# A graph-network kernel whose gathers signal VectorE: each group's five VectorE operations begin on that signal, in another order, and the sums are copied with a lag of one group

## What is computed

```
h = maximum(layernorm(x), 0)
eq = h @ Wq + bq
ek = h @ Wk + bk
e = edge_attr @ We + be
m = relu(eq[dst] + ek[src] + e)
ft = segment_sum(m, dst, num_segments=6250)
out = x + ft @ Wr + br
```

## Time and profile before

| what | value |
|---|---|
| median of 3 runs | 1306.76 us (1306.44 to 1307.97) |
| profiled execution, first to last instruction | 1303.3 us |
| edge phase in it, first gather to last | 118.4 to 1230.8 us |
| busy in the whole span | PE 1153.0, DVE 964.9, ACT 841.4, POOL 948.3 us |
| DMA | 303.48 MB, mean 233 GB/s |

### The profile page before, as it was taken

How to read it: one execution, slowest core, us unless ns; L and a number is a source line. 1 busy time by engine, 2 the same in 40 slices (tenths; PEclk the granted TensorE clock), 3 DMA queues, 4 the chain that set the end, 5 groups by cost and what they waited for, 6 DMA issues and landing times.

```text
span 1303.3 us, 33240 instructions
## 1 busy us (share of the span) xinstructions
PE 1153.0 (88%) x8632; PEld 1056.0 (81%) x8632; DVE 964.9 (74%) x1324; ACT 841.4 (65%) x1463; POOL 948.3 (73%) x946
## 2 busy tenths in 40 slices
PE   2997899999999999999989898999999989999776
PEld 2776888888888888888888888888888888888766
DVE  6885777777777777777777777777777777777688
ACT  2775676666666666666666666666666666666533
POOL 4545777777777777777777777777777777777644
PEclk9998999999999999999999999999999999999989
DMA  8887877777777777777777777777777777777564
GB/s 263 287 285 245 248 230 233 230 233 230 235 234 244 228 235 231 235 233 233 237 233 235 233 232 232 232 232 231 230 235 234 242 224 240 230 233 232 191 188 149
DMA packets 164469, 303.48 MB, mean 233 GB/s; under 512 B 29204, under 2 KB 110740, under 8 KB 164452
## 3 DMA queue, kind: packets, MB, share of 16 engines
q1 hardware_dynamic: 124516, 194.18, 45.7%
q0 software_dynamic: 39936, 109.11, 28.8%
HBM read 275.69 MB, written 27.48 MB: 233 GB/s over the span
## 4 chain that ended last, share of the span: by engine, by line
POOL 53%; issue 32%; PE 8%; DVE 3%; DMA 2%; POOLq 1%; ACT 1%; DVEq 0%; SPq 0%; ACTq 0%
POOL k_rows L492 53%; PE p_sum L926 4%; PE p_edge L926 3%; DVE hT_lo L888 1%; DMA ft<-in_x 1%; PE p_turn L935 1%; POOLq L499 0%; POOLq L237 0%; DMA pre<-in_dst_groups 0%; DMA range_table<-top_g 0%; DVE k_rows L900 0%; DMA rel_row<-rel_table 0%; DMA k_rows<-k_table,idx 0%; DVE k_rows L715 0%; POOLq L490 0%
## 5 line engine op out<-in xcount | busy, mean ns | idle before, releaser
L492 POOL DMA_INDIRECT k_rows<-k_table,idx x832 | 859.1, 1033 | 256.1 <-issue 255.5
L926 PE MATMUL p_edge<-we_hi,edge_hi 128*128 128x256 f32 x1664 | 487.5, 293 | 27.0 <-issue 17.9
L835 DVE TENSOR_TENSOR pre<-p_edge,k_rows 128x1024 f32<-128x1024 f32 x208 | 254.6, 1224 | 300.9 <-issue 155.4
L926 PE MATMUL p_edge<-we_lo,edge_hi 128*128 128x256 f32 x1664 | 466.4, 280 | 0.0
L926 PE MATMUL p_edge<-we_hi,edge_lo 128*128 128x256 f32 x1664 | 466.0, 280 | 0.0
L612 ACT ACTIVATE m_hi<-pre 128x1024 fp32r<-128x1024 f32 x208 | 221.0, 1062 | 352.0 <-DVE pre L835 351.8
L926 PEld LDWEIGHTS p_edge<-we_hi,edge_hi 128*128 128x128 f32 x1664 | 315.3, 189 | 61.2 <-issue 57.4
L926 PEld LDWEIGHTS p_edge<-we_lo,edge_hi 128*128 128x128 f32 x1664 | 316.1, 190 | 0.0
L926 PEld LDWEIGHTS p_edge<-we_hi,edge_lo 128*128 128x128 f32 x1664 | 314.1, 189 | 0.0
L843 DVE SCALAR_TENSOR_TENSOR m_lo<-pre,m_hi 128x1024 fp32r<-128x1024 f32 x208 | 254.3, 1223 | 1.7 <-ACT m_hi L612 1.7
L816 DVE TENSOR_TENSOR edge_lo<-edge,edge_hi 128x1024 fp32r<-128x1024 f32 x208 | 252.7, 1215 | 0.9 <-ACT edge_hi L591 0.9
(11 more groups left out here) (81 smaller groups left out, 961.1 us busy)
## 6 DMA issues: line engine op xcount, KB each, us to landing
edge<-in_edges SPq DMA_DIRECT2D x208, 512.0 KB
rel_row<-rel_table SPq DMA_DIRECT2D x208, 96.0 KB
q_win<-q_table SPq DMA_DIRECT2D x416, 48.0 KB
q_table<-m_hi SPq DMA_DIRECT2D x52, 256.0 KB, 2.5
k_rows<-k_table,idx POOLq DMA_INDIRECT x832
ft<-in_x SPq DMA_DIRECT2D x4, 1664.0 KB, 11.8
k_table<-k_rows SPq DMA_DIRECT2D x52, 128.0 KB, 3.0
out_rows<-k_rows SPq DMA_DIRECT2D x13, 512.0 KB, 3.2
```

The costliest lines, as they stand in the source:

```text
L492: nc.gpsimd.indirect_dma_start(out=k_rows[:, slot, j, :], out_offset=None, in_=k_table, in_offset=bass.IndirectOffsetOnAxis(ap=idx[:, slot ...
L835: nc.vector.tensor_tensor(pre[:, slot % 2, :], p_edge[:, slot % 2, :], k_rows[:, slot].rearrange("p t d -> p (t d)"), ALU.add).then_inc(s_ ...
L926: ins = nc.tensor.matmul(target, a(h), b[:, h, :], start=(h == 0 and n == 0), stop=(stop and h == HALVES - 1 and n == 2))
```

## The change

```diff
+LEAD = 2
+        s_wrote = sem("gather_descriptors_written")
...
                     nc.gpsimd.indirect_dma_start(
                         out=k_rows[:, slot, j, :], out_offset=None, in_=k_table,
                         in_offset=bass.IndirectOffsetOnAxis(ap=idx[:, slot, j:j + 1], axis=0),
+                        engine_sem=s_wrote,
                     ).then_inc(s_rows[slot], 16)
...
                     message_high(it, u)
                     if not (last and u + 2 >= UNROLL):
                         make_pick(it, u + 2)
-                    if not (first and u < 2):
-                        take_sum(it, u - 2)
+                    if not (first and u < 1):
+                        take_sum(it, u - 1)
...
             steps(bodies - 1, last=True)
-            take_sum(bodies - 1, UNROLL - 2)
             take_sum(bodies - 1, UNROLL - 1)
...
-            def add_rows(it, u):
+            def add_rows(it, u, last=False):
                 body, slot, n, _, _ = visit(it, u)
 
+                if not (last and u + LEAD >= UNROLL + 1):
+                    dve.wait_ge(s_wrote, TILES * (n + LEAD))
                 after(dve, s_prod, n)
                 dve.wait_ge(s_rows[slot], 16 * TILES * (body + 1))
                 after(dve, s_mlo, n - 2)
...
             def steps(it, first=False, last=False):
                 for u in range(UNROLL):
-                    add_rows(it, u)
+                    add_rows(it, u, last)
+                    make_send(it, u)
+                    if not (first and u < 3):
+                        add_sum(it, u - 3)
                     if not (last and u + 2 >= UNROLL):
                         edge_low(it, u + 2)
-                    make_send(it, u)
                     message_low(it, u)
-                    if not (first and u < 3):
-                        add_sum(it, u - 3)
```

## The result

The changed kernel takes 1419.4 us (median of 4 runs, 1418.28 to 1419.53), the kernel before beside it 1306.6 us (median of 4, 1306.1 to 1307.97). The ratio is 1.0862, interval 1.0846 to 1.0878: 8.6% slower. The forecast of 1275 us and its range up to 1310 were wrong. The rival "the signal is too early", priced at 1424 us, is what happened.

What follows compares the result with a forecast made beforehand. POOL's 832 back-to-back gathers were taken as the bound, 5.35 us per group. A mean period of 5.19 us saved 33 us, 2 us came back: 1306.8 - 31 = 1275 us, range 1260 to 1310.

Steps and rivals of the forecast that it cites:

- the signal is too early: Rival on the new wait: p under 0.055 us lets `m_lo` hold up third gathers; 115 us more, 1424 us; chance 0.19.
- What s is: Step estimating when `pre` starts after the awaited gather: 0.17 us, giving a period of 5.05 us, bounds 5.03 to 5.21.
- p: Time from a gather's profiled end until POOL counts it as finished; taken as 0.14 us, possible from 0 to 0.305.
- s: Start of `pre` on DVE, counted from the end of the fourth gather whose signal it awaits; taken as 0.17 us.
- steps 1 to 3: Edge-loop steps where the wait stands on `pre` itself; predicted period 5.05 us each.
- The contention: DVE operation with two SBUF inputs running 0.05 us into a gather delays its end to 0.83 us after that operation; 66 us overall.
- No contention to be won: Rival from the skill's inference: DVE's order would not matter to gathers, time about 1308 us; chance 0.02.
- The seam: Point between `edge_lo` and `m_lo` where the third gather comes in; needs s over 0.085 us.
- The period: Time per group of four gathers: the larger of 5.03 us and s + 4.88 us.
- step 0: Edge-loop step with its wait three instructions ahead of `pre` and late `edge_lo`, 0.27 us each; predicted 5.59 us.
- the rest: Side effects: ACT's copy lag costs nothing, PE stays 0.14 us short of bounding, 2 us added once at the end.
- the late rival: Rival on the new wait: p of 0.22 to 0.305 us uses up the gain, 1293 to 1309 us; chance 0.18.

Runs made afterwards that it cites:

- wait-last kernel: Changed kernel, new wait behind `pre`'s others, one instruction after it in steps 1 to 3: full 1254.9 us; light (16 of 24 edge-product matmuls left out) 1255.1 us.
- light counting: Kernel before without 16 of its 24 edge-product matmuls, gathers counted in `s_wrote` and nobody waiting: 1314.0 us, ratio 1.0053 to the full kernel before.

## Why the prediction was wrong

**The step that failed is "What s is".** It took p = 0.14 us between a gather's profiled end and the signal, and so s = 0.17. In the changed kernel `pre` starts 0.033 us (0.032 to 0.034 in steps 1 to 3) after the gather's end. The way to DVE alone, 0.03 us by the earlier trace rows for an ordinary POOL operation, accounts for all of that, and less than 0.01 us is left for p. The row I went by has POOL's sequencer at its next instruction 0.14 us after a gather's end; the signal reaches DVE 0.1 us before that, so the row bears on something else. Rows 6 spoke for the early signal with the very number, and got 0.19.

Everything that hangs on s was right, once s is put in:

- **The contention** (a look soon after the start, an end 0.83 us after the DVE operation's). Gathers of 1.965, 1.65, 1.10, 1.00 and 1.13 us in four kernels end where it says. Only the look at 0.05 us is too strict for an operation that does not follow another with two SBUF inputs: the second gather of the changed kernel has `edge_lo` begin 0.04 us after its start (707.82 against 707.78) and stays at 0.95 us. The Trainium skill, "SBUF — State Buffer", section "Who interferes with whom", infers that `tensor_tensor` does not hold up descriptor writing. The traces do not agree for these gathers: with `edge_lo`, a `tensor_tensor`, running at its start the gather takes 1.65 in place of 0.95 us. "No contention to be won" fell with it.
- **The seam**, s over 0.085. s = 0.033 loses it and s = 0.145 keeps it. No kernel had an s between the two, but the 0.05 us on which the threshold rests is borne out by the other seams above.
- **The period** s + 4.88: 5.12 measured for s = 0.245, and for step 0 of the wait-last kernel 0.033 + 0.27 + 4.88 = 5.18 against 5.206. For the lost seam 6.05 was priced, 6.043 measured; step 0 5.46, measured 5.480.
- **`edge_lo` after `pre`**: 1.58 and in step 0 1.85; measured 1.571 and 1.858. The three instructions ahead of `pre` in step 0: 0.27; measured 0.312 - 0.033 = 0.28.
- **The sum of the rival**: 208 x 5.90 = 1227 us of edge phase, measured 1225.0.

Of "the rest": counting is free, shown by light counting. That PE is not the bound at 5.03 us is shown by the two wait-last kernels, light and full, with the same time, though PE leads the chain of the full one. The 2 us at the end did not come: from the last gather's end to the last instruction it takes 72.6 us after and 72.5 before. `pre` of the last group is 0.7 us later, not 2: it starts 3.5 us after the last gather's end, and before it started 2.8 after it, where the prediction had about 2. Behind it, the shorter lag leaves three `ft` after the last `m_lo` in place of four, which the prediction did not count. The lag of ACT's copy was not tried alone; nor was the new order alone on a chip where POOL bounds.

The weighing of the late rival was wrong as well: 0.18 for p of 0.22 to 0.305 rested on "the 0.30 us gap must hold something". Whatever it holds, the signal does not wait for it.

## What to carry to other kernels

A wait that lines one engine up with another fixes a phase between them, and a fixed phase repeats its luck in every round: the old order lost 0.32 us per group to the contention, the new one 1.01 us in three groups of four. When a result turns on a few hundredths of a microsecond, price both sides of the edge, take the signal's delay from the nearest completion of the same engine and not from what its sequencer does next, and put in a cheap instruction to move the phase before giving the idea up. That a change is slower may mean that it stands 0.1 us from its best place.

## What the runs showed of the hardware

- The completion of a gather reaches a waiting DVE operation 0.033 us after its profiled end, while the next gather starts 0.305 us after it; nothing in these runs says what fills that gap.
- The place of a wait in the queue is a delay of its own: 0.033 us on the operation itself, 0.146 to 0.153 with one semaphore instruction between, 0.242 to 0.249 when the operation's other waits pass behind it too, 0.31 with three sequencer instructions between, in step 0.
- A gather can be more than doubled, 0.95 to 1.97 us, by two DVE operations with two SBUF inputs back to back, if the boundary between them falls 0.01 us after its start, and not at all if it falls 0.12 us after. The edge is at 0.05 us, or, by the start of the operation that holds the gather up, at 0.03 us before the gather's start.
- The same kernel took 1307 us on some chips and 1701 to 1734 us on others, with TensorE's granted clock at 0.85 and stretches in which PE stood nearly still. There the kernels with the signal and the shorter lag were 6 to 7% faster whatever the phase, with a granted clock of 0.88 to 0.91. What makes these chips differ is left open.
